# FFN loop of a ViT-tower kernel: transposes of the normalised rows and all four score products between the second and the third weights product

## What is computed

```python
q = (x @ Wq + bq).reshape(-1, N_HEADS, D_KEYS)       # 8 heads, 128
q1, q2 = (q[..., :HALF], q[..., HALF:])
s1 = jnp.einsum('bhc,hnc->bhn', q1, keys[:, 0])      # scores against 64 keys
s2 = jnp.einsum('bhc,hnc->bhn', q2, keys[:, 1])
s1t, i1 = lax.top_k(s1, TOP_K)                       # TOP_K = 8
s2t, i2 = lax.top_k(s2, TOP_K)
all_scores = s1t[..., :, None] + s2t[..., None, :]
scores, best = lax.top_k(all_scores, TOP_K)          # indices into 64*64 rows
inner = jnp.einsum('bd,bhkd->bhk', x, w_down[indices])
vals = jax.nn.relu(inner) * jax.nn.softmax(scores, axis=-1)
out = jnp.einsum('bhk,bhkd->bd', vals, w_up[indices])
```

## Time and profile before

| | us |
|---|---|
| runs | 7798.26, 7819.33, 7841.44 |
| the profiled execution, its own time | 7833.56 |
| its span, first to last instruction | 7831.7 |
| PE busy | 6593.8 (84%) |
| DVE busy | 6650.3 (85%) |
| ACT busy | 3258.4 (42%) |
| GpSimd busy | 1886.3 (24%) |
| mean granted TensorE clock | 0.888 |

### The profile page before, as it was taken

One profiled execution on the slowest core, in us unless ns is written; L12 is line 12 of the kernel. 1 busy time (PEld: TensorE's weight loads), 2 busy tenths in 40 slices (PEclk: granted clock), 3 DMA queues, 4 the chain that ended last, 5 costly groups with the idle time before them and its releaser, 6 DMA issues. The chain is left out here.

```text
span 7831.7 us, 210914 instructions
## 1 busy us (share of the span) xinstructions
PE 6593.8 (84%) x81726; PEld 5036.9 (64%) x81726; DVE 6650.3 (85%) x24235; ACT 3258.4 (42%) x6997; POOL 1886.3 (24%) x2655
## 2 busy tenths in 40 slices
PE   8798899889999989547777777678898898899898
PEld 8566666666666666335555555457777777777777
DVE  1688877887777778689999999879999999999998
ACT  0355555555555555335555555422222222222221
POOL 0222222222222222234444444410110110111010
PEclk9799998998998999768888888879999999999898
DMA  7434343343333444000000000000000000000000
GB/s 209 51 52 61 55 56 52 58 59 56 52 52 52 54 57 58 14 4 5 5 5 5 5 5 5 18 23 11 11 9 11 11 9 11 11 9 11 11 9 9
DMA packets 335660, 245.52 MB, mean 31 GB/s; under 512 B 36150, under 2 KB 333401, under 8 KB 334332
## 3 DMA queue, kind: packets, MB, share of 16 engines
q1 hardware_dynamic: 334716, 232.82, 18.2%
HBM read 61.50 MB, written 13.04 MB: 10 GB/s over the span
## 5 line engine op out<-in xcount | busy, mean ns | idle before, releaser
L580 DVE TENSOR_REDUCE negmax<-S 99x4 f32<-99x788 f32 x1024 | 997.6, 974 | 412.0 <-PE S L344 408.9
L467 ACT ACTIVATE probs<-ST 99x792 f32<-99x792 f32 x1024 | 850.4, 830 | 713.3 <-PE ST L354 701.5
L1393 PE MATMUL f_IN<-f_zT,f_wd 128*128 128x256 f32 x3200 | 827.5, 406 | 0.6 <-ACT f_act L1470 0.6
L1405 PE MATMUL f_AA<-f_hotp,f_hot 64*128 64x32 bf16 x38400 | 549.6, 175 | 281.9 <-DVE f_act L1667 234.7
L1405 PEld LDWEIGHTS f_AA<-f_hotp,f_hot 64*128 64x128 bf16 x38400 | 513.1, 94 | 383.1 <-issue 365.7
L344 PE MATMUL S<-ks,qs 96*99 96x198 bf16 x4096 | 597.2, 272 | 188.6 <-DMA ks<-parts 134.4
L1418 PEld LDWEIGHTS f_OT<-f_wu,f_act 128*128 128x128 f32 x6400 | 732.4, 192 | 6.0 <-issue 0.9
L1418 PE MATMUL f_OT<-f_wu,f_act 128*128 128x128 f32 x6400 | 732.9, 275 | 0.8 <-issue 0.8
L344 PEld LDWEIGHTS S<-ks,qs 96*99 96x99 bf16 x4096 | 409.4, 136 | 447.6 <-DVE negmax L580 160.9
L1393 PEld LDWEIGHTS f_IN<-f_zT,f_wd 128*128 128x128 f32 x3200 | 596.0, 198 | 147.5 <-issue 50.8
L879 PE MATMUL a_SC<-a_kT,a_qm 128*128 128x198 f32 (+1 forms) x1716 | 501.0, 458 | 197.9 <-ACT a_kT L957 173.9
(11 more groups left out here) (185 smaller groups left out, 12874.3 us busy)
## 6 DMA issues: line engine op xcount, KB each, us to landing
qs<-parts SPq DMA_DIRECT2D x768, 99.0 KB, 3.9
ks<-parts SPq DMA_DIRECT2D x768, 99.0 KB, 4.6
xbuf<-x_in SPq DMA_DIRECT2D x64, 588.0 KB, 4.5
f_hx<-tokens SPq DMA_DIRECT2D x50, 128.0 KB, 3.2
f_hr<-tokens SPq DMA_DIRECT2D x50, 128.0 KB, 3.2
out<-f_hr SPq DMA_DIRECT2D x50, 128.0 KB, 1.8
qs<-mrows SPq DMA_DIRECT2D x256, 9.3 KB
tokens<-h SPq DMA_DIRECT2D x64, 49.5 KB
```

The lines of the kernel that those rows point to most:

```text
L467: A.activation(probs[:, p].rearrange("p h k w -> p h (k w)"), ST[:, :, 0:2 * W], ACT.Exp, scale=float(HD) ** -0.5).then_inc(st_taken, 1)
L580: V.tensor_reduce(negmax[:, j, :, 2 * p:2 * p + 2].rearrange("p q h -> p h q"), S[:, :, 0:2 * W].rearrange("p h (q k) -> p h q k", q=2)[:, ...
L1393: mm = nc.tensor.matmul(IN[k % 2][:, m * STEP:m * STEP + STEP], wd[:, 2 * k + m, :], zT[:, par, :], start=True, stop=True)
L1405: mm = nc.tensor.matmul(AA[slot][c][:, t * NP:t * NP + NP], hot[64 * c:64 * c + 64, g % 2, tt // TL, :, tt % TL], hotp[64 * c:64 * c + 64, ...
```

## The change

In each step PE turns the normalised tokens after the second weights product, as before, and then does all four score products at once. Before, one score product followed each of the third to sixth weights product. The inner products of the next step, before in blocks of 2, 2, 2, 2, 2 and 3 behind the third to eighth weights product (the last 3 follow in the next step), stand in blocks of 4, 4 and 5 behind the fourth, sixth and eighth. ACT's copies follow the same order. Nothing is added or left out, and DVE's and GpSimd's programs stay as they are.

```diff
-INNER = (0, 2, 4, 6, 8, 10, 13, 16)
+INNER = (0, 0, 4, 4, 8, 8, 13, 16)
@@ PE
                     if has2:
                         if u == 1:
                             turn_z(n + 2)
-                        elif 2 <= u < 6:
-                            scores(n + 2, par, u - 2)
+                            for k in range(4):
+                                scores(n + 2, par, k)
@@ ACT
                 for u in range(2, UNITS):
-                    if has2 and 2 <= u < 6:
-                        copy_scores(n + 2, par, u - 2)
+                    if has2 and u == 2:
+                        for k in range(4):
+                            copy_scores(n + 2, par, k)
```

## The result

The changed kernel takes 7955.24 us (median of four runs, 7947.88 to 7963.93) against 7830.39 us for the kernel before in the same session: 124.9 us more by medians. By the interval it is slower by 1.5 to 2.1%, 113 to 160 us. The prediction said 7937 us, in a range of 7765 to 8060, with 68% on slower. The profiled execution took 7959.69 us; the sum had said 7951.

A forecast was written before the change was run, and what follows sets the result against it. Each step's chain was taken to run on DVE up to the third weights product, then on PE alone. Terms -1.9 + 2.0 + 2.3 gave +2.4 us a step, +118 in 50 steps: 7937 us, range 7765 to 8060.

The forecast's parts named there:

- the sum: Whole kernel: -1.9 + 2.0 + 2.3 = +2.4 us a step, +118 us in 50 steps, 7951 us profiled.
- The gap: Scores moved into PE's gap before the third weights product: DVE's waits nearly all go, -1.9 us a step, -95 in all.
- The bound of 112.2 us: DVE's waits for weights products (77.1 us) and turned indices (35.1): the most any new order on PE could give back.
- The scores at half clock: Four score rounds at half clock delay the third weights product: mean of 0 and 3.9, +2.0 us a step, +100.
- The pairs: Three new pairs of weights products a step, half halting for instructions at 1.5 us: +2.3 us a step, +113.
- The 3.9 us for a fetch: Instruction fetch, read from the last step's weights products: about 1.78 + 2.12 us; 254 instructions passing faster must halt.
- The first: Rival: gap simply filled, halts fall into PE's slack, clock stays up in the scores; 7707 to 7725 us; 19%.
- The rule that the fetch is hidden: Skill's rule for PE's instruction fetches: hidden by the ~20-cycle issue floor, so the new pairs' halts would cost 0.
- the third term: Halts for instructions in the three new pairs of weights products: +2.3 us a step, +113.
- the second rival: Over the step, terms cancel: clock costs half, halts half hidden, -1.9 + 1.0 + 1.1, about 0; 7780 to 7858 us; 13%.
- The cascade: Rival: every scores stretch at half clock, halts keep it down through inner products; +6.1 us a step, 8124 us; 16%.

The follow-up runs named there:

- the scores alone: Against the kernel before: four score products together behind the turned tokens, inner products in their old places, no new pair; 7875.22 us, ratio 1.0081.
- e_best: Against the kernel before: two score products and three inner blocks in PE's gap, third and fourth weights product paired, other scores behind fourth and sixth; 7668.36 us, ratio 0.9813.
- the pairs alone: Against the kernel before: third to eighth weights product in three pairs, each score product ahead of two inner blocks behind a pair; 7962.34 us, ratio 1.0184.
- the light kernel: Against the kernel before: weights products with one of three parts plus eight wide overwritten products; 7863.03 us in the old order, 7719.18 in the changed order.
- e_mix: Against the kernel before: two score products with an inner block between in PE's gap, two behind third and fourth weights product, no new pair; 7709.89 us, ratio 0.9865.

## Why the prediction was right

**The gap (-1.9 us a step): too much.** The 35 to 41 us of waits for the indices went as forecast in the scores alone (to 7.9). But most of the waits for weights products is the 62.2 us at the fourth, in 48 steps, and it stays where one score product is moved (76.5) or two with a block between (46.1). Behind the third product of the earlier trace rows the score product runs at half clock:

```profile
6575.71 2.07 PE L1371 MATMUL f_WK<-f_wc,f_zT 128*128 128x512 f32 x2
```

So the fourth comes late; e_best, with nothing between the third and the fourth product, has none of this wait. With the scores alone the indices gave 33.5 us and the seventh and eighth product 15.8 (21.6 before, 5.8 then): some 49 us, half of the 95 that I counted. I had -95 + 100 = +5 us for the scores; alone they cost 45 to 83. The bound of 112.2 us for any order was too low as well: e_best took 153 us off. In its profile the loop is 143.5 us shorter, 114.8 of them in DVE's two waits, of which the whole loop had 125.9, and 22.9 in DVE's own busy time, for which no run here gives a reason.

**The scores at half clock (+2.0): right.** 56% of the score products at half clock, where I took half; the third product's wait 113.8 us, 2.3 a step. Without a halt and at full clock the third product starts 11.3 us after the first, for 11.4 forecast.

**The pairs (+2.3, 75 halts of 1.5 us): right as a sum of halts, too low as a cost.** In the second to fourth pair there were 106 halts inside products, of 130.4 us, in 150 pairs: 1.23 us each. Before, there were 15.2 us at these places, so 115 us are new, for 113 forecast. More halted than half, and each was shorter than in a first pair (26.8 us in 20). But 115 us are the length of the halts and not their price: the pairs alone, with 115 us of new halts too, cost 122 to 165 us, and the clock fell with them, which the forecast had only at the end of its range. The 3.9 us for a fetch hold in the last step, where two fetches start 3.89 us apart; in the loop they come as close as 3.2 us.

**Why the sum still came out.** Both mechanisms are there as forecast, but that the sum is so near is in part luck. I had +5 us for the scores and +113 for the pairs; alone they cost 54.7 and 141.8. That they give back 72 us when they stand together is nowhere in the forecast, and it made good what both terms lack. In the change DVE waits at the third product (113.8 us), the fourth (23.1), the seventh (40.1) and for the indices, whose wait I had let go: it rose to 116.7 us. What the runs show is +163 us in the loop of the profiles and 113 to 160 in the runs, for 118 forecast.

**The rivals.** The first, faster by 95 to 112 us, needed kind fetches and a kind clock: with no halts and little half clock, the light kernel in the changed order is 144 us faster than in the old, and e_mix, with neither new pair nor pauses, 80 to 131 us faster than before. Its mechanism was right, and its conditions did not hold. The rule that the fetch is hidden (the Trainium skill, Runtime: NRT & Kernel Launch, Instruction fetch mechanics) is not borne out, by 159.5 us of issue waits in the profile after, each of which ends behind a fetch. The prediction also took the wrong rival for that rule: without the third term its sum is -1.9 + 2.0, about 0, which is the second rival's. The cascade did happen in single steps (up to 61.4 us), not in the mean (56.9).

## What to carry to other kernels

When products are put in a row, count instructions as well as time: here PE halted where a block of 256 ran out before the next one was there, and in the last step the blocks came 3.9 us apart, where small matmuls with a load each pass one in 1.8. A gap on TensorE is worth filling, but with independent work between products that wait for each other's copy; the same four score products cost 0.8% with pauses and gained 0.7% with an inner block in each. Pauses did harm above all behind a halt, so look at both together. And a halt is judged by who waits behind it: 62 us of them in a pair that stood where PE was early made DVE wait for nothing.

## What I had not expected of the hardware

In the change a halt in a new pair was a little shorter (1.23 us) than in the first (1.34) or in the last step (2.12), although less seemed to be queued ahead of it. It is no rule of new pairs: with the pairs alone their halts took 1.61 us in the mean (first pair 1.27), and in the new pair of e_best 1.64. What sets the length stays open. Eight wide bf16 products (256 columns) take 1.86 us at half clock and 1.04 at full, while 96 small ones with their loads take 1.47 and 1.37: an order that costs PE its clock hardly touches those, and doubles the fp32 products beside them. How much of the gain of the light kernel is the fetch and how much the clock no run takes apart.
